# A fused attention and feed-forward kernel: first and last work units replanned, and half 0 of the last unit's probabilities turned by flips and DMAs

## The reference, cut to what matters

```
x = x + attn(layernorm(x), W_Q, W_K, W_V, W_O)      # x: 2 x 1024 x 256, 16 heads of 128, causal softmax
x = x + (layernorm(x) * gamma + beta) @ ternary(weight).T + bias    # weight 256 x 256

attn:    scores = q @ k.T / sqrt(128), masked above the diagonal
         out = sum over heads of softmax(scores) @ v @ W_O
ternary: clip(round(w / (mean(abs(w)) + 1e-5)), -1, 1)
```

## Time and profile before

| | us |
|---|---|
| three runs | 816.1, 816.5, 816.52; median 816.5 |
| the profiled execution | 813.95, its span 811.9 |
| TensorE busy | 801.7 (99%) |
| VectorE, ScalarE, GpSimd busy | 666.5, 557.1, 547.4 |

### The profile page before, as it was taken

One profiled execution on the slowest core, in us unless ns is written; L12 is line 12 of the kernel. 1 busy time (PEld: TensorE's weight loads), 2 busy tenths in 40 slices (PEclk: granted clock), 3 DMA queues, 4 the chain that ended last, 5 costly groups with the idle time before them and its releaser, 6 DMA issues.

```text
span 811.9 us, 14642 instructions
## 1 busy us (share of the span) xinstructions
PE 801.7 (99%) x4846; PEld 722.6 (89%) x4846; DVE 666.5 (82%) x1470; ACT 557.1 (69%) x1031; POOL 547.4 (67%) x280
## 2 busy tenths in 40 slices
PE   8999999999999999999999999999999999999998
PEld 7988998888999898899888899888889888899887
DVE  8988787888787878878878878788878788878988
ACT  6877667667666667666766766766766766766684
POOL 6188755696666856768557885568665686676486
PEclk9999999999999999999999999999999999999999
DMA  6366766456656565666655676546656655555603
GB/s 189 82 147 146 176 140 142 117 132 170 141 137 143 137 153 128 138 151 149 162 124 119 149 175 144 140 108 146 167 132 143 145 128 130 130 137 137 144 13 105
DMA packets 57226, 111.49 MB, mean 137 GB/s; under 512 B 16960, under 2 KB 21184, under 8 KB 57152
## 3 DMA queue, kind: packets, MB, share of 16 engines
q1 hardware_dynamic: 57152, 110.56, 57.0%
HBM read 10.88 MB, written 2.10 MB: 16 GB/s over the span
## 4 chain that ended last, share of the span: by engine, by line
PE 92%; DVE 3%; SPq 2%; DMA 1%; POOL 1%; issue 1%; ACT 0%; POOLq 0%; ACTq 0%
PE scores L701 23%; PE ring L654 23%; PE ring L634 21%; PE ring L643 11%; PE ring L664 10%; SPq L452 2%; PE ring L673 1%; DMA pT<-turn 1%; PE ring L598 1%; PE scores L763 1%; POOL norm L544 1%; DVE acc L878 1%; DVE stats L896 0%; PE scores L691 0%; DVE scores L858 0%
## 5 line engine op out<-in xcount | busy, mean ns | idle before, releaser
L528 POOL TENSOR_TENSOR pT<-pT 128x1024 fp32r<-128x1024 f32 x186 | 444.7, 2412 | 251.7 <-ACT pT L799 251.6
L792 ACT ACTIVATE turn<-scores,negmax 128x128 f32<-128x128 f32 (+7 forms) x256 | 189.0, 739 | 154.5 <-DVE negmax L858 88.3
L858 DVE CUSTOM_DVE_ANT_0 scores<-scores,mask 128x128 f32<-128x128 f32 (+7 forms) x256 | 192.7, 763 | 101.7 <-PE scores L701 100.5
L701 PE MATMUL scores<-kT,qT 128*128 128x512 f32 (+2 forms) x1056 | 224.9, 350 | 1.2 <-ACT turn L792 1.2
L654 PEld LDWEIGHTS ring<-pT,v 128*128 128x128 f32 x1116 | 188.0, 189 | 24.8
L654 PE MATMUL ring<-pT,v 128*128 128x512 f32 x1116 | 209.8, 342 | 0.0
L799 ACT ACTIVATE pT<-pT 128x1024 fp32r<-128x1024 f32 x186 | 196.4, 1057 | 16.3 <-DMA pT<-turn 15.4
L701 PEld LDWEIGHTS scores<-kT,qT 128*128 128x128 f32 x1056 | 175.5, 188 | 20.6 <-ACT turn L792 2.2
L866 DVE STREAM_TRANSPOSE turn<-turn 128x128 f32<-128x128 f32 (+1 forms) x248 | 187.1, 764 | 0.0
L664 PE MATMUL ring<-wo_s,zT 128*128 128x256 f32 x768 | 113.3, 284 | 0.2 <-DVE zT L929 0.2
L878 DVE SCALAR_TENSOR_TENSOR acc<-ring,inv,acc 128x256 f32<-128x256 f32 x256 | 109.5, 469 | 0.0
(11 more groups left out here) (84 smaller groups left out, 553.4 us busy)
## 6 DMA issues: line engine op xcount, KB each, us to landing
pT<-turn SPq DMA_DIRECT2D x496, 128.0 KB, 2.3
pT<-turn SPq DMA_DIRECT2D x496, 64.0 KB, 2.0
acc<-in_x SPq DMA_DIRECT2D x8, 256.0 KB, 5.3
wk_raw<-in_wk SPq DMA_DIRECT2D x8, 256.0 KB, 2.9
wq_raw<-in_wq SPq DMA_DIRECT2D x8, 256.0 KB, 3.8
wv_raw<-in_wv SPq DMA_DIRECT2D x8, 256.0 KB, 3.0
norm<-in_wo SPq DMA_DIRECT2D x8, 256.0 KB, 2.9
out<-acc SPq DMA_DIRECT2D x8, 256.0 KB, 2.2
```

The lines of the kernel that those rows point to most:

```text
L528: pool.tensor_tensor(chunk(half, LO, c), f32(chunk(half, LO, c)), f32(chunk(half, HI, c)), ALU.subtract).then_inc(plo_ready, 1)
L701: mm = pe.matmul(scores[:, t % 2, first + c:first + c + n], qT[:, par, a, t * P:(t + 1) * P], kT[:, par, m, c:c + n], start=(i == 0), stop ...
L792: act.activation(turned, columns, ACT.Exp, bias=negmax[:, t % 2:t % 2 + 1], scale=-1.0, accum_out=rowsum[:, u % 2, t:t + 1]).then_inc(prob ...
L858: dve.tensor_tensor_reduce(out=tile, in0=tile, in1=mask[:, S - (t + 1) * P:S], scale=-1.0, scalar=FAR, op0=ALU.add, op1=ALU.min, accum_out ...
```

## The change

- `TURNS` and `GROUPS` lose half 0. In the last unit, half 0 now goes as in the others: flips, four waves (16 DMAs), hip, lop, and a "pv" 0 31. `last_probs` loses its branch for half 0.
- The START and END tables of TensorE, ScalarE, VectorE and GpSimd have a new order, SP's END table has the four waves; the five steady tables and SP's START table are as they were. The lists of jobs in START are the same apart from 30 for 34 warming matmuls (50 for 48 at the very start).
- "norm2" 0 to 3 move from GpSimd to ScalarE.
- GpSimd builds the identity before the mask, with a semaphore of its own, and clears `turn1` after the first three weight splits.
- "bw" takes beta split by GpSimd into both parts ("beta"): four matmuls in the reduced format for two in full single precision.
- "ff" 7, its add and its store go in two halves of one tile each.

```diff
-WARM_UP = 48
+WARM_UP = 50
...
-TURNS = (((0, 0, 1), (1, 0, 2)), ((2, 0, 3),), ((3, 0, 4),), ((4, 0, 4),), ((4, 4, 1), (5, 4, 2)), ((5, 0, 4),),
-         ((6, 0, 4),), ((6, 4, 3),), ((7, 0, 4),), ((7, 4, 4),))
+TURNS = (((4, 0, 4),), ((4, 4, 1), (5, 4, 2)), ((5, 0, 4),), ((6, 0, 4),), ((6, 4, 3),), ((7, 0, 4),), ((7, 4, 4),))
...
-GROUPS = ((0, 4), (4, 2), (6, 2))
+GROUPS = ((4, 2), (6, 2))
...
 END_SYNC = (
...
+    ("wave", 1, 2, 30), ("wave", 1, 3, 30), ("wave", 0, 0, 31), ("wave", 0, 1, 31), ("wave", 0, 2, 31),
+    ("wave", 0, 3, 31), ("out", 0), ("out", 1), ("out", 2), ("out", 3), ("out", 4), ("out", 5), ("out", 6),
+    ("out", 7, 0), ("out", 7, 1),
...
 START_GPSIMD = (
-    ("clear", 1), ("split", "k", -1), ("split", "q", -1), ("split", "v", -1), ("lop", 0, 0, 0), ("lop", 0, 1, 0),
+    ("split", "k", -1), ("split", "q", -1), ("split", "v", -1), ("clear", 1), ("lop", 0, 0, 0), ("lop", 0, 1, 0),
...
-                if u < LAST:
+                if u < LAST or half == 0:
                     columns = columns.rearrange("p (j b i) -> p j b i", b=A, i=Q)
...
-                    pe.wait_ge(small_in, 48)
-                    for kd in range(KD):
-                        mm = pe.matmul(dst[:, 0:D], beta_s[:, kd:kd + 1].broadcast_to([P, P]), f32(wf_s[:, kd, :]),
-                                       start=(kd == 0), stop=(kd == KD - 1))
+                    pe.wait_ge(beta_ready, 2)
+                    for i, (kd, a) in enumerate([(kd, a) for kd in range(KD) for a in (LO, HI)]):
+                        mm = pe.matmul(dst[:, 0:D], beta_r[:, a, kd:kd + 1].broadcast_to([P, P]), wf_s[:, kd, :],
+                                       start=(i == 0), stop=(i == 3))
...
-            pe.wait_ge(const_ready, 6)
+            pe.wait_ge(ident_ready, 3)
```

More of the change, by code:

```diff
@@ L199, in exists @@
             return u % KINDS == (2 if item[1] == "v" else 3) and u < LAST - 1
-        return kind != "load"
+        if kind in ("flip", "wave", "hip", "lop", "pv"):
+            return 0 <= u < LAST
+        return 0 <= u <= LAST and kind != "load"
     def run_of(start, table, end):
@@ L398, in split_target, with last_probs @@
             return [(hi, lo, bank[:, 0:n * P], None)]
[L400 to L404 removed]
+        def last_probs(part, j0, n):
             if part == HI:
@@ L414, in last_turn, with tiles_of, own_tiles @@
             return flat[:, t % HALF * keys:t % HALF * keys + (t + 1) * P]
+        def tiles_of(item):
+            c = item[1]
+            if len(item) == 3:
+                return (2 * c + item[2],)
+            return tuple(2 * c + j for j in range(2) if item + (j,) not in vector_norm)
+        def own_tiles(item):
+            return (item[2],) if len(item) == 3 else (0, 1)
         def wait_norm(engine, item):
@@ L495, in _ @@
                 else:
-                    store(item[1])
-            sp.wait_ge(stored, 16 * (NT // 2))
+                    store(item)
+            sp.wait_ge(stored, 16 * sum(i[0] == "out" for i in sync_run))
         @block.gpsimd
         def _(pool):
+            pool.memset(ident[:, :], 0.0).then_inc(ident_ready, 1)
+            pool.wait_ge(ident_ready, 1)
+            pool.affine_select(out=ident[:, :], in_=ident[:, :], compare_op=ALU.not_equal, fill=1.0, base=0,
+                               pattern=[[-1, P]], channel_multiplier=1).then_inc(ident_ready, 1)
+            pool.wait_ge(ident_ready, 2)
+            pool.tensor_copy(ident_b[:, :], ident[:, :]).then_inc(ident_ready, 1)
+            own = mask[:, S - P:S]
             pool.memset(zero, 0.0).then_inc(const_ready, 1)
-            pool.memset(ident[:, :], 0.0).then_inc(const_ready, 1)
             pool.memset(mask[:, :], 0.0).then_inc(const_ready, 1)
-            own = mask[:, S - P:S]
-            pool.wait_ge(const_ready, 3)
-            pool.affine_select(out=ident[:, :], in_=ident[:, :], compare_op=ALU.not_equal, fill=1.0, base=0,
-                               pattern=[[-1, P]], channel_multiplier=1).then_inc(const_ready, 1)
+            pool.wait_ge(const_ready, 2)
             pool.affine_select(out=own, in_=own, compare_op=ALU.is_ge, fill=MASKED, base=0,
                                pattern=[[-1, P]], channel_multiplier=1).then_inc(const_ready, 1)
-            pool.wait_ge(const_ready, 4)
-            pool.tensor_copy(ident_b[:, :], ident[:, :]).then_inc(const_ready, 1)
             splits = [0]
@@ L614, in last_weighted_v @@
                 first, n = GROUPS[g]
-                half, hh = first // HALF, LAST % 2
+                hh = LAST % 2
                 for j in range(first + n):
@@ L666, in project_o, with project_ffn @@
                 return mm
-            def project_ffn(c, dst):
-                for j in range(2):
+            def project_ffn(c, own, dst):
+                for j in own:
                     tok = (2 * c + j) * P
@@ L673, in project_ffn @@
                         mm = pe.matmul(dst[:, j * D:(j + 1) * D], xT[:, a, kd, tok:tok + P], wf_s[:, kd, :],
-                                       start=(j == 0 and i == 0), stop=(i == 3), skip_group_check=True)
+                                       start=(j == own[0] and i == 0), stop=(i == 3), skip_group_check=True)
                 return mm
```

99 lines of the change are left out of this document (55 added, 44 removed), and 48 rows, old and new, of tables (END_SCALAR, END_TENSOR, END_VECTOR, START_TENSOR).

## The result

The changed kernel takes 819.03 us (median of 6 runs, 818.15 to 819.62); the kernel before took 815.43 us (6 runs, 814.55 to 816.52). The ratio is 1.0043, with a 95% interval of 1.0028 to 1.0059: slower by some 3.6 us. The forecast was 818.4, from the 816.5 then known, in a range of 813.0 to 820.2. So sign and range held, but the move was put at +1.9 us and is +3.6 against the kernel before as measured beside it. That 818.4 and 819.03 lie so close is in part luck: the kernel before came out 1.1 us under the 816.5 that the forecast started from.

The account below looks back on a forecast made before the run. It took TensorE (busy 99%) as the bound, VectorE at the end. End +1.9, start -0.1 or -1.2, stretched issue 0 or +1.1 gave +1.9 us as likeliest: 818.4 from 816.5, range 813.0 to 820.2.

Parts of the forecast that it names:

- The start: Before the first qk: saves 1.2 us if VectorE's shift comes ahead of GpSimd's instruction, otherwise 0.1; even chances.
- TensorE's savings ahead of score tile 6 become waiting: Unit 31: score tile 6 still starts at 774.0, so TensorE's saved work turns into waits at s 2, s 4, s 6.
- SP's queue: End: unit 30's DMAs fill SP's queue until 771.19; 16 added issues end at 781.3, the last landing at 782.7.
- added issue was stretched: End, SP: one of the sixteen added issues is held in about half of the executions, costing 0 or 1.1 us.
- pv 1 30 1.25 us earlier, pv 0 31 at 787.0, exp 7 late: End: pv 1 30 starts at 777.4, pv 0 31 at 787.0; exp 7 delays tp 3 for VectorE to 787.5.
- The end, +1.9: VectorE's last add 2.1 us later, from 2.65 us more work and 2.0 of waits; smaller last store 0.2 back.
- The sign that the prediction named: End: if right, VectorE's last add comes some 37 us behind s 6; wrong if at or under 35.2 us.
- four cases of the sum: Whole kernel: combinations of start, end and stretched issue, +0.7, +1.8, +1.9 and +3.0 us; the middle ones likeliest.
- At this point VectorE sets the end: From pv 1 30's low half on, VectorE's list, busy 23.20 of 24.53 us before, sets the end, not TensorE.
- TensorE as the bound of the end: Rival, end: the tables hold and TensorE stays the bound; 811.5 us, half of it 814; chance 0.20.
- the two ends cancelling: Rival: start -1.2, no stretched issue, VectorE's waits no longer than before; +0.0, 816.5 us; chance 0.14.
- The longer chain: Rival, end: DMA near its limit, exp 7 later still, each microsecond reaching the end; +4, 820.5 us; chance 0.08.

Follow-up runs that it names:

- e11: The changed kernel measured once more, unaltered: 818.30 us, ratio 1.0047 to the kernel before.
- e9: The kernel before with the new start, and norm2 1 in its old end made by ScalarE instead of GpSimd: 813.81 us, ratio 0.9991.
- e1: The kernel before with only the changed kernel's start (tables, 50 warming matmuls, identity first): 814.53 us, ratio 0.9999.
- e4: The changed kernel with exp 7 of unit 31 moved up on ScalarE, ahead of the square-root table: 820.91 us, ratio 1.0071 to the kernel before.
- e7: e3 with three TensorE products (o 0 29, o 3 29, o 1 30) made twice: 818.22 us, ratio 1.0050 to the kernel before.
- e5: e3 with VectorE's adds for o 0 31 and o 1 31 cut to one column: 818.27 us, ratio 1.0047 to the kernel before.
- e10: e5 with GpSimd's two low halves of unit 31's half 0 formed over half their columns: 816.45 us, ratio 1.0024 to the kernel before.
- e2: The changed kernel with the old start (tables, 48 warming matmuls, old order of mask and identity): 819.43 us, ratio 1.0050 to the kernel before.
- e3: The changed kernel with VectorE's shifts of two or four columns written as single-column instructions: 817.63 us, ratio 1.0034 to the kernel before.
- e6: e3 with TensorE making one of three passes of pvl 0 and pvl 1: 817.30 us, ratio 1.0037 to the kernel before.

## Why the prediction was right, and where it was not

**The start** was forecast at -0.1 or -1.2. In the profile it gave -0.55. Where the shift runs free the first qk comes at 10.41 (e11), 10.50 (e9) and 10.70 (e1); 10.45 had been worked out. What failed is the sentence that GpSimd's splits "start 0.1 us earlier at most": they started 0.64 us earlier, at 5.63, and at 5.34 to 6.55 in the other kernels with the new start. So two values were too few, and the first qk at 11.04 lies between them: it is a race against transfers, those of the weights and of the input. With the old form of the shift the mark at exp 0 of unit 2 moved by anything between +0.34 (e4) and -1.06 us (e9). The Trainium skill's rule (page "SBUF — State Buffer", section "🔬 SBUF: two separate sides"), an exclusive lock of the shared port pair held for the whole instruction, with a VectorE op of two SBUF inputs on one side of it: the traces agree, as five held shifts end within 0.03 us of GpSimd's instruction (11.03 and 11.00 before; 10.38 and 10.37, 800.54 and 800.53, 808.57 and 808.56 here; 791.52 both in e9). The rows also show the order: every held shift began after GpSimd's instruction, and shifts that began just ahead of one took 0.16 us (5.52 against 5.63 here, 797.93 against 797.97 before).

**Steady units unchanged**: right for the work, as e1 and e11 show. That their time wanders by up to 2.5 us from one profiled execution to another was not in the working; it is why the profiles differ by 5.6 us and the medians by 3.6. Start -0.55 and end +4.0 give +3.4 by themselves.

**TensorE's savings ahead of score tile 6 become waiting**: right. The waits were put at s 2 (1.3 us), s 4 and s 6; they are 0.88, 0.83 and 1.11. Score tile 6 starts 20.15 us behind pv 1 29, before 20.32. e7 shows it from the other side.

**SP's queue**: its 48 issues end 27.45 us behind pv 1 29's start (first issue at 751.47, 31.26 us for all, pv 1 29 at 755.28); the forecast 781.3 is 27.6 on the same scale. The wave was to land at 782.7, 29.0 behind; e5 saw it at 28.8, e10 at 29.2. In the changed kernel itself hip 0 1 31 was not released by it, since ScalarE reached it at 784.32, 29.0 behind, from pv 1 30. No added issue was stretched (the longest of the 48 took 1.44 us and is one of unit 30's, as the 1.71 before), so that term is 0 here. Of nine profiles with the new end two have one among the added issues, 1.15 us in e5 and 1.08 in e10, and in these two hip 0 1 31 waits for its wave; it had been put at half of the executions and 1.1 us.

**pv 1 30 1.25 us earlier, pv 0 31 at 787.0, exp 7 late**: pv 1 30 starts 23.67 behind, forecast 23.7. Its low half is done 29.8 behind, forecast 29.7. pv 0 31 starts 33.2 behind, forecast 33.3. Exp 7 starts 32.3 behind; the chain as worked out (wave 782.7, then 1.0, 0.9 and 1.28) gives 32.2. Right.

**The end, +1.9**, is the term that was mis-sized; it measured +4.0. Behind pv 1 30's low half the working had 23.2 + 2.65 of VectorE's work and 2.0 of waits, 27.85 us; measured are 29.58. Of the difference of 1.73 us, 1.4 are the held shifts (four shifts took 2.2 us instead of 0.8), 0.15 are waits, the rest work. Then 0.1 us was passed on from the gate, and the last store as two halves gave 0.1 us away instead of 0.2 back. The step that failed is one that was not taken: the lock was weighed in the start, where the trace of before showed it, and not in the end, where each of GpSimd's eight bias adds, on two tensors of SBUF, now waits for a norm of ScalarE, and two of them are under way when VectorE's shifts come. Four profiles (changed, e11, e2, e4) have both, at 1.14 to 1.15 and 0.69 to 0.70 us. e3 takes the holding away and ends 0.8 us earlier, with 0.7 us of new instructions in its place. The sign that the prediction named misses by as much: the last add was to come some 37 us behind score tile 6, and comes 39.2 behind (before: 35.2).

Two of the four cases of the sum are 0.1 us too high as added up (0.7 + 1.1 is 1.8, and 1.8 + 1.1 is 2.9); it changes nothing in the result.

**"At this point VectorE sets the end"** holds only from pvl 0 on (e5). The sum of work and waits ahead of pvl 0 came out near all the same, because that part of the list filled time in which the chain through exp 7 ran: the 1.1 us that e5 took from the work came back as waiting. That part of the agreement is luck, and what of the 2.65 us of added work costs time is not shown.

**The rivals.** TensorE as the bound of the end is out by e6; the two ends cancelling is out by e2. The longer chain (+4) is nearest in size, but its mechanism is not what added the 2 us over the forecast: exp 7 came where the forecast had it.
